# Four graph layers on one core: all row gathers of a pass issued by GpSimd

## The reference, cut to what matters

```
x = ln(x + GRU_L0(x))     # 4 steps: m = x @ W_msg.T + b (4 kinds of edge); r = segment_sum(m[src, kind], dst); x' = gru(r, x)
x = ln(x + SAGE_L1(x))    # pe = relu(w @ pos_w1) @ pos_w2; s = segment_sum(pe * x[src] + x[src], dst); mean, linear, batchnorm
x = ln(x + GRU_L2(x))     # segment_sum(x[src] @ W.T + emb[kind], dst); gru
x = ln(x + ATT_L3(x))     # attention over the edges of each dst, with k[src] and v[src]; norm; feed forward
```

## Time and profile before

| | us |
|---|---|
| median of 3 runs | 4273.61 |
| lowest and highest | 4272.66, 4279.78 |
| span of the profiled execution | 6447.3 |
| PE busy in it | 2897.1 |
| GpSimd busy in it | 2764.1 |
| DVE busy in it | 1811.8 |
| ACT busy in it | 443.4 |

### The profile page before, as it was taken

The page is one execution under the profiler, slowest core; times in us unless marked ns, Lnnn a source line. Parts: engine busy times, 40 slices in busy tenths (PEclk is TensorE's granted clock), DMA queues, the critical chain, the costliest instruction groups (busy, mean ns, idle before and its releaser), DMA issues. The chain is left out here.

```text
span 6447.3 us, 67941 instructions
## 1 busy us (share of the span) xinstructions
PE 2897.1 (45%) x12174; PEld 2182.6 (34%) x12175; DVE 1811.8 (28%) x4739; ACT 443.4 (7%) x719; POOL 2764.1 (43%) x2883
## 2 busy tenths in 40 slices
PE   5443044441064430365632555567444106555578
PEld 3333023331033320133421454455333004545465
DVE  3222021221032220233321322223222005555685
ACT  2000010000010000100000100002000001000133
POOL 4666016663056660166630444452666203665400
PEclk7776567665576665677766678778677557766789
DMA  3111011110011110111110111110111001433331
GB/s 114 47 47 45 3 43 46 46 47 23 3 64 47 47 44 3 39 48 45 45 29 9 46 31 32 31 36 27 43 47 48 18 3 62 128 123 119 97 126 54
DMA packets 167915, 315.16 MB, mean 49 GB/s; under 512 B 63863, under 2 KB 89662, under 8 KB 167138
## 3 DMA queue, kind: packets, MB, share of 16 engines
q0 software_dynamic: 94528, 207.40, 12.3%
q1 hardware_dynamic: 60818, 102.68, 4.7%
q10 hardware_dynamic: 12304, 2.65, 0.2%
HBM read 250.84 MB, written 61.65 MB: 48 GB/s over the span
## 5 line engine op out<-in xcount | busy, mean ns | idle before, releaser
L708 POOL DMA_INDIRECT ring<-m_tab,idx x1536 | 1470.2, 957 | 812.2 <-issue 435.9
L1689 PE MATMUL ps<-oh,ring 128*128 128x256 f32 (+1 forms) x2902 | 885.1, 464 | 1913.3 <-DMA ring<-m_tab 994.8
L1689 PEld LDWEIGHTS ps<-oh,ring 128*128 128x128 f32 x2902 | 640.4, 243 | 2041.1 <-issue 1946.9
L1689 PE MATMUL ps<-nodes,ring 128*128 128x256 f32 (+1 forms) x2766 | 820.9, 454 | 731.7 <-issue 619.8
L1174 DVE TENSOR_SCALAR oh<-iota,dl 128x256 f32<-128x256 f32 x1248 | 386.5, 381 | 2432.4 <-PE ps L1689 1397.4
L708 POOL DMA_INDIRECT ring<-x_tab,idx x768 | 729.5, 950 | 611.7 <-PE ps L1689 311.5
L1689 PEld LDWEIGHTS ps<-nodes,ring 128*128 128x128 f32 x2766 | 593.7, 237 | 844.5 <-issue 759.1
L1174 DVE TENSOR_SCALAR nodes<-iota,dl 128x256 f32<-128x256 f32 x1175 | 364.6, 380 | 982.6 <-remote 913.2
L708 POOL DMA_INDIRECT ring<-kv_tab,idx x416 | 403.5, 970 | 262.8 <-DVE rec L1485 136.5
L728 POOL TENSOR_TENSOR small<-small,bc 128x4 f32<-128x4 f32 (+1 forms) x28 | 29.6, 1056 | 967.1 <-DVE small L1273 967.1
L540 POOL TENSOR_TENSOR ring<-nodes,ring 128x512 f32<-128x512 f32 (+1 forms) x21 | 24.3, 1155 | 897.0 <-ACT ring L820 897.0
(11 more groups left out here) (261 smaller groups left out, 2646.1 us busy)
## 6 DMA issues: line engine op xcount, KB each, us to landing
ring<-m_tab SPq DMA_DIRECT2D x4096, 0.5 KB
ring<-m_tab ACTq DMA_DIRECT2D x4096, 0.5 KB
ring<-x_tab SPq DMA_DIRECT2D x2048, 0.5 KB
ve_dr<-pw SPq DMA_DIRECT2D x52, 512.0 KB
ring<-ve_dr SPq DMA_DIRECT2D x52, 512.0 KB, 3.4
ring<-m_tab,idx POOLq DMA_INDIRECT x1548
m_tab<-ring SPq DMA_DIRECT2D x75, 256.0 KB, 2.2
ring<-x_tab ACTq DMA_DIRECT2D x1024, 0.5 KB
```

Source lines behind the costliest of these rows:

```text
L708: pool.indirect_dma_start(rows[:, j, :], None, table, bass.IndirectOffsetOnAxis(ap=idx[:, wave * WV + j:wave * WV + j + 1], axis=0)).then_ ...
L1689: return T.matmul(o, lhsT, rhs, start=start, stop=stop, skip_group_check=True)
```

## The change

GpSimd fetches all 403 tiles of a pass of L0, L1 and L2, in plain order, with `ring`'s four waves as the only buffer. The rows fetched by SP and ACT, their row numbers and their semaphores are gone, and so are the far slots, the orders written by hand and the split of wave 47. DVE and PE go over waves 0 to 47 in a loop of 12 turns of four, and over waves 48, 49 and 50 after it. `wpad` is loaded behind the first table. L3 is as it was.

```diff
-LOOPED = FULL // DEPTH - 1
+LOOPED = P_WAVES // DEPTH
+P_REST = P_WAVES - LOOPED * DEPTH
...
+IN_SLOT = [16 * sum(tiles_of(wave) for wave in range(s, P_WAVES, DEPTH)) for s in range(DEPTH)]
+def landed(k, s, i, n=WV):
+    return k * IN_SLOT[s] + i * (16 * WV) + 16 * n
...
-            for p, wave in enumerate(LAST_POS):
-                body(LOOPED, p, wave, tiles_of(wave))
+            for u in range(P_REST):
+                body(LOOPED, u, LOOPED * DEPTH + u, tiles_of(LOOPED * DEPTH + u))
...
-        def sp_rows(sp, table, at):
-            far_rows(sp, mybir.EngineType.SP, table, at[0], 0, SP_TILES, x_sp)
-        def act_rows(act, table, at):
-            far_rows(act, mybir.EngineType.Activation, table, at[1], SP_TILES, ACT_TILES, x_ac)
...
                 for n in range(WIN):
-                    if n == BY_POOL:
-                        sp.wait_ge(xi_st, 16)
-                        row_numbers(sp, 0)
...
             first_table(m_rows)
-            sp.wait_ge(xi_ld, 32)
-            for s in range(STEPS):
-                for b in range(RING):
-                    sp.wait_ge(mt_dma[b], (s + 1) * (16 * MT_SLOTS[b]))
-                sp_rows(sp, m_tab, xrow0)
-                if s == 0:
-                    keep_numbers(sp, 1)
-                if s + 1 < STEPS:
-                    table(s + 1, m_rows, 512)
+            sp.dma_start(wpad_flat, a["wpad"]).then_inc(s_wpad, 16)
+            for s in range(1, STEPS):
+                table(s, m_rows, 512)
...
-                waves, deep, slots = (WAVES, RING, SLOTS) if single(k) else (FULL, DEPTH, NEAR)
+                waves, deep, slots = (WAVES, RING, SLOTS) if single(k) else (P_WAVES, DEPTH, P_SLOTS)
...
-                    if k == PASS_L1 and g == L1_THEN_ACT:
-                        for t in range(SP_TILES, SP_TILES + ACT_TILES):
-                            pool.indirect_dma_start(
-                    if slots == NEAR and g == (FULL - 1 if k == PASS_L1 else LOOPED * DEPTH - 1):
-                        for t in range(SP_TILES + ACT_TILES, FAR):
-                            pool.indirect_dma_start(
...
-                hidden(s, "L0", m_landed(s))
-                act_rows(act, m_tab, xrow0)
+                hidden(s, "L0")
                 evac(s)
...
-            for n, (to, i_) in enumerate(zip(x_bytes, (idx4, idx1))):
-                step(f"i_x{n}", V.tensor_scalar(to, i_[:, NEAR:NEAR + SP_TILES + ACT_TILES], 9, None, ALU.logical_shift_left))
```

More of the change, by code:

```diff
@@ L122, in first_wave, with tiles_of @@
     return k * P_WAVES
[L125 to L139, removed]
+def tiles_of(wave):
+    return P_LAST if isinstance(wave, int) and wave == P_WAVES - 1 else WV
+IN_SLOT = [16 * sum(tiles_of(wave) for wave in range(s, P_WAVES, DEPTH)) for s in range(DEPTH)]
+def landed(k, s, i, n=WV):
+    return k * IN_SLOT[s] + i * (16 * WV) + 16 * n
 class Any1(dict):
@@ L268, in build @@
         credit = sem("credit")
-        gat = [sem(f"gat{i}") for i in range(DEPTH)]
+        gat = [sem(f"gat{i}") for i in range(max(DEPTH, RING))]
         mt_mm = sem("mt_mm")
@@ L313, in build @@
         b_e2 = sem("b_e2")
[L314 to L317, removed]
         s_wpad = sem("s_wpad")
-        gat_end = sem("gat_end")
-        x_sp = [sem(f"x_sp{i}") for i in range(4)]
-        x_ac = [sem(f"x_ac{i}") for i in range(4)]
         b_used = sem("b_used")
@@ L386, in build @@
                  + [yT[:, 1024 * b:1024 * (b + 1)].rearrange("p (s c) -> p s c", c=P) for b in range(2)])
-        x_bytes = [pw[:, 1, 32 * j:32 * j + SP_TILES + ACT_TILES].bitcast(I32) for j in range(2)]
         cntc, inv = small[:, 208:208 + WIN], small[:, 176:176 + WIN]
@@ L406, in slot @@
             return ring[:, s % RING, :, h:h + D]
[L408 to L415, removed]
         def halves(wave):
@@ L425, in split_turns @@
                     body(i, u, i * DEPTH + u, WV)
-            for p, wave in enumerate(LAST_POS):
-                body(LOOPED, p, wave, tiles_of(wave))
-        X_SP, X_AC = (n * P // 4 * 16 for n in (SP_TILES, ACT_TILES))
-        def far_slot(t):
-            return ring[:, t // WV, t % WV, D:2 * D]
+            for u in range(P_REST):
+                body(LOOPED, u, LOOPED * DEPTH + u, tiles_of(LOOPED * DEPTH + u))
         def wave_rows(wave, u):
-            if isinstance(wave, int) and wave >= FULL:
-                return ring[:, wave - FULL, :, D:2 * D]
@@ L439, in wave_rows @@
             return slot(wave % DEPTH if isinstance(wave, int) else u)
[L441 to L460, removed]
@@ L498, in arrived @@
                 eng.wait_ge(gat[u], landed(k, u, i))
[L499 to L508, removed]
+            else:
+                eng.wait_ge(gat[wave % DEPTH], landed(k, wave % DEPTH, wave // DEPTH, tiles_of(wave)))
         def logit_turns(eng, body):
@@ L529, in whole_turns @@
         def whole_turns(eng, turn):
-            with eng.Fori(0, LOOPED - 1) as i:
+            with eng.Fori(0, LOOPED) as i:
                 turn(i, [i * DEPTH + u for u in range(DEPTH)])
-            turn(LOOPED - 1, L1_POS)
+            turn(LOOPED, [LOOPED * DEPTH + u for u in range(P_REST)])
         def new_state(unit, eng, r, c, h_in, h_out):
@@ L635, in rows_out @@
                     sp.dma_start(dst, buf).then_inc(ln_dma[c % 2], 16)
[L637 to L641, removed]
             rows_out(0)
@@ L710, in gathers @@
                             bass.IndirectOffsetOnAxis(ap=idx[:, wave * WV + j:wave * WV + j + 1], axis=0)
-                        ).then_inc(gat_end if slots == NEAR and g == FULL - 1 and j >= LAST_SPLIT else gat[u], 16)
-                    if k == PASS_L1 and g == L1_THEN_ACT:
-                        for t in range(SP_TILES, SP_TILES + ACT_TILES):
-                            pool.indirect_dma_start(
-                                far_slot(t), None, table,
-                                bass.IndirectOffsetOnAxis(ap=idx[:, NEAR + t:NEAR + t + 1], axis=0)).then_inc(x_l1, 16)
-                    if slots == NEAR and g == (FULL - 1 if k == PASS_L1 else LOOPED * DEPTH - 1):
-                        for t in range(SP_TILES + ACT_TILES, FAR):
-                            pool.indirect_dma_start(
-                                far_slot(t), None, table,
-                                bass.IndirectOffsetOnAxis(ap=idx[:, NEAR + t:NEAR + t + 1], axis=0)).then_inc(x_pl, 16)
+                        ).then_inc(gat[u], 16)
             def norm(ln):
@@ L797, in evac, with hidden @@
                     nc.scalar.activation(gT[:, c0:c0 + cw], ps[:, c, 0:cw], ACT.Copy).then_inc(ev_a, 1)
-            def m_landed(s):
-                def f():
-                    for b in range(RING):
-                        act.wait_ge(mt_dma[b], (s + 1) * (16 * MT_SLOTS[b]))
-                return f
-            def hidden(r, L, landed=None):
+            def hidden(r, L):
                 parts = len(hid[L])
@@ L808, in hidden @@
                     c0, cw = CH[n // parts]
-                    if n == parts * NCH - 1 and landed:
-                        landed()
                     act.wait_ge(hid_mm, r * (3 * NCH) + (n + 1))
@@ L853, in _ @@
                     gru(s, "L0", c)
-            hidden(STEPS - 1, "L0", m_landed(STEPS - 1))
-            act_rows(act, m_tab, xrow0)
+            hidden(STEPS - 1, "L0")
             evac(STEPS - 1)
@@ L896, in _ @@
             hidden(STEPS, "L2")
-            act.wait_ge(xi_ld, 64)
-            for c in range(2):
-                act.wait_ge(ln_dma[c], LN_DMA(2, c))
-            act_rows(act, x_tab[1], xrow)
             evac(PASS_L2)
@@ L1371, in messages @@
                         arrived(dve, PASS_L1, i, u, wave)
-                        if hf and isinstance(wave, int) and wave == FULL - 1:
-                            all_arrived(dve, PASS_L1)
                         dve.wait_ge(l1_pe, (i * DEPTH + u) * 2 + (hf + 1))
@@ L1752, in wave @@
                     for j in range(n):
-                        if isinstance(g, int) and g == FULL - 1 and j == LAST_SPLIT:
-                            all_arrived(pe, k)
                         ins = mm(psf[:, ds(cs[j], PAIR)], wave_rows(g, u)[:, j, :], pair_oh(u, j), start=False, stop=False)
```

22 lines of the change are left out of this document (removed).

## The result

| | before | after |
|---|---|---|
| median us, 4 runs each on one chip | 4276.06 | 4369.12 |
| lowest and highest | 4272.66, 4279.78 | 4366.43, 4371.13 |
| span of the profiled execution | 6447.3, in a second profile 4273.4 | 4369.0 |

The change makes the kernel slower: the ratio is 1.0218, 95% interval 1.0203 to 1.0232, or +93 us. The forecast was +101.

What follows compares the result with a forecast made beforehand. The prediction took GpSimd's issue of gathers to bound all seven passes. From 4273.6 us, 88 more gathers add 109.9 and the earlier first gather takes off 8.4, giving 4375 us, range 4332 to 4413.

Steps and rivals of the forecast that it cites:

- Spacing as the price: Passes of L0, L1, L2: each of 88 added GpSimd gathers costs its start-to-start spacing, 1.249 us, together +109.9 us.
- B: Gathers in most passes: GpSimd waits for credit, so extra gathers fill waits; no change, 4265 to 4278; chance 0.05.
- C: Gathers still bound the passes but cost 0.944 us each, nothing for L1; 4341 us; chance 0.08.
- Rows hidden: SP's and ACT's 11264 row transfers lie behind GpSimd's 483 us a pass, so removing them gives 0.
- the slow rate: Rows beside gathers in the first profile: 1.42 us each on SP, 1.28 on ACT; mostly absent from timed runs.
- The check: Seven passes: 2746 gathers at 1.249 make 3429.8 us of the timed 3490.9, leaving 61.1, or 8.7 us a pass.
- Order and tail: Pass ends: plain order and different last tiles change nothing; 0 taken, within -2 and +3 us a pass.
- ACT's lateness: Pass ends: if ACT's rows end late in each of five passes, removing them gives back up to 50 us.
- First table: Start: without SP's wait for row numbers the first gather moves from 67.2 to about 58.8, -8.4 us.
- The sum: Whole kernel: 4273.6 + 109.9 - 8.4 = 4375.1, so 4375 us (+2.4%).
- What the profile would show: Six passes of 403 gathers 1.249 us apart, no 270 us row waits, first gather near 59, span some 1200 us shorter.
- Rival D: Ends of six passes: without the hand-made order each ends one PE wave later; 4395 to 4412 us; chance 0.11.

## Why the prediction was right

The time (4375 for 4369.12) and the mechanism hold: GpSimd's issue bounds every pass. Step by step:

- *Spacing as the price.* 88 x 1.249 = 109.9 was said, +111.7 measured (81.3 + 10.0 + 20.4). The kernels with 8, 40 and 88 gathers more all pay 1.18 to 1.27 us each in the trace. Rivals B (hidden, at most 4278) and C (0.944 us each, 4341) are out, and with B the 4265 that the prediction drew from the Trainium skill (DMA: Bandwidth & Descriptors, "Anatomy of one DMA — SWDGE (gpsimd) path").
- *Rows hidden.* Right in time: 88 large transfers in place of all rows give 0.1% (0.02 to 0.2%). The prediction asked whether ACT's rows end in time, and they do (539.9 for a last gather at 550.5, and PE takes their wave without a wait). What it left out is what rows do to the gathers beside them: these land up to 15 us late, and the four waves of `ring` cover it. The reasoning from the earlier trace rows to the timed runs was right: the slow rate was the odd execution's.
- *The check.* It closed to 8.7 us a pass, partly by luck, since its terms came from the odd execution. It took 782.7 us for all that lies outside the passes, and the second profile has 4273.4 - 3537.1 = 736.3. The passes are thus 3537.1 and not 3490.9, their gathers 3453.5 and not 3429.8, and the ends 83.6 and not 61.1. With L3's 32.5 us end left out, an ordinary end is 8.5 us, so the conclusion stands on the better numbers too.
- *Order and tail.* Mis-sized: 0 was taken, -12.6 measured, 5.7 of it in L1. It was argued by PE's time for a wave; in L1, where the chain is only 6% faster than GpSimd, the order decides what is still queued at the last gather. L1 in plain order shows this part alone. In L0's last pass the order counts too: 12.4 with the hand-made one and no rows, 7.3 in after, while before and its variants have 9.9 to 14.6. In the first and third pass the 8.1 and 6.8 of before come from wave 46 at a lower granted clock, not from ACT's lateness; after has 5.7 and 5.5. These few microseconds differ between executions: before's six ends sum to 51.1 in this one, and to 52.9 and 54.6 in the kernels that only move the row numbers.
- *First table.* -8.4 was said from 67.2 to 58.8. The first gather is at 59.1, but before starts at 65.9 in the second profile, so -6.8; by the eight profiles that keep the wait it is -5.7 to -11.6. The prediction put the cost down to SP's wait alone, and there its mechanism was incomplete. Taking the wait away left 63.75; with the numbers' small writes out of the table's way too it is 60.24. With a start that varies by 6 us the two shares are rough.
- *The sum.* 109.9 - 8.4 = +101.5 against 111.7 - 6.8 - 12.6 + 3.3 = +95.6. The price of the gathers was near, the small terms were off by up to 12.6 us and offset each other.
- *What the profile would show.* 403 gathers 1.25 us apart, no wait for rows, a first gather near 59: all there. The span did fall, but by 2078 and not 1200 us, and that it fell was luck: the prediction said that the slow rows go with the change, and the second profile of before keeps every row and spans 4273.4. All 2174 us of the excess belonged to the odd execution, not to the rows.
- *Rival D.* The reverse is true: with GpSimd as the only fetcher the hand-made order's ends are 24 us longer than the plain one's by the traces, 19 of them in L1. It was made for rows that land early.

No kernel tried beats the one before by more than its own interval lets one say; of those that compute the whole, row numbers read behind the table come nearest (0.9995, 0.9986 to 1.0004).

## What to carry to other kernels

When a span is far from the timed runs, multiply the instructions of the engine that seems to be the bound by their start-to-start spacing before believing any wait, compare that with the timed run, and ask for a second profile. Where an engine that issues one indirect transfer after another is the bound, as here, each costs its start-to-start spacing, and work moved to it from idle queues is paid nearly in full (+93 us for 110). Work that fills idle queues must end earlier than the bound by the time of whatever is queued behind it, and an order made by hand for early data turns against the kernel once that data comes late. Transfers that look free can delay the landing of others, and then it is the depth of the buffer that hides them.

## What the runs showed of the hardware

- A plain 512-byte transfer with its address from a register costs SP 0.41 to 0.42 us and ACT 0.43 to 0.44 us, beside GpSimd's gathers or (in the first profile) without them, and does not change the gathers' spacing (1.2528 us in the first pass with 2048 of them beside, 1.2516 with 16 large ones, 1.2538 with none).
- Such rows do delay the gathers' landing where both engines issue them: PE starts a wave 15 us after its last gather in place of 1.8 us, at the same spacing. With SP's rows alone it stays at 1.8 us.
- The same sixteen matmuls took 3.72, 5.40 and 6.74 us at a granted clock of 1.00, 0.68 and 0.54, the second and third after PE had stood 3.0 and 2.8 us. Standing 2.8 us came before the 3.72 as well.
- A write of 8 KB in 4-byte pieces takes 11.8 us, and 256 KB writes issued around it on another queue land in 7.2 us (median of 11) instead of 2.1 (of 12).
- One profiled execution of twelve was stretched by half (6447.3 for 4273.4 us), at a granted clock of 0.70 where the second shows 0.82. What caused it stays open.
